# Differential attention of 8 heads: two value steps together behind score 4, the others behind scores 10 and 12

## The chip, the cores and the metric

The kernel runs on one core of a Trainium2 chip. Its time is the device time of one execution in microseconds (us). The core's engines work side by side, each through its own instruction stream in order: TensorE (PE, its weight loads PEld), VectorE (DVE), ScalarE (ACT), GpSimd (POOL) and SyncE (SP, which issues DMAs). They hand work to each other through semaphores.

## The reference

The program is a stack of twelve layers on an input of 4 batches x 512 tokens x 128 channels. The change lies in the eleventh, the differential attention of layer L3: 8 heads, each with two score maps of 8 dimensions, and the second softmax is subtracted with the weight `diff_weight`:

```python
qs = (x @ Wq.T).reshape(b, s, H, 2, F)          # H = 8, F = 8
ks_ = (x @ Wk.T).reshape(b, s, H, 2, F)
vs = (x @ Wv.T).reshape(b, s, H, DH)            # DH = 16
scores = jnp.einsum('bqhif,bkhif->ibhqk', qs, ks_) * scale
atts = jax.nn.softmax(scores, axis=-1)
att = atts[0] - diff_weight * atts[1]
o = jnp.einsum('bhqk,bkhe->bqhe', att, vs)
```

The result is normalised over all channels, projected by `Wo` and added to the stream.

## The kernel before

`diff_attention(kind)` serves two layers; kind 3 is the one with 8 heads, kind 2 the one with 16. In kind 3 the work comes in 16 items (4 batches x 4), each of 4 maps (two heads, two maps each) over 512 queries x 512 keys. The softmax is computed with the true maximum of each row subtracted, and that takes two passes over the scores:

- **Peaks.** `peak(n, i)` (L2090) computes a 128 x 512 block of scores of item n, 16 blocks per item, into one of three PSUM banks (`PEAKS = 3`, L1945). DVE takes the maximum of each row (`reduce`, L2387). Peak i must wait until the reduction of peak i-3 is done. Peaks run 24 blocks (`LEAD`), that is one and a half items, ahead of the scores.
- **Placing.** POOL writes the negated maxima as bfloat16 columns into NM (`negate`, L2551 and L2553), once all 16 reductions of an item are done. PE adds them to the stacked queries through identity matmuls (`place`, L2117 and L2119, two per item) and ACT copies the result to QM (`shift`, L2283).
- **Scores.** `score(n, i)` (L2129), again 16 blocks per item, writes the shifted scores with the keys on the partitions into a ring of four PSUM banks, which placings, gatherings and projections share; ACT takes the exponential into EX (L2276).
- **Values.** `value(n, c)` (L2139), c = 0 to 3, multiplies a quarter of the exponentials by the values, in float32, four maps side by side in column tiles of 32. A step shows in the trace as 8 matmul records. All four steps of an item accumulate into bank 4. They run one item late: during item n the steps of item n-1.
- **Gathering.** ACT takes bank 4 to OT (`take`, L2290), PE turns it (`gather`, L2150), and DVE copies the turned block to OS (`keep`, L2022), once per item from item 2 on. DVE works through its own order: `keep` stands ahead of the ninth reduction of an item.

The loop over an item on PE has 16 places i = 0 to 15. At each stand, in this order: the peaks that `AHEAD_OF` puts there, score i, a placing of the next item (i = 10 and 12), a gathering (i = 6), in items 0, 4 and 8 a projection of the next batch (i = 3 and 7), and a value step where `AT_VALUE` says so. In this text P0 to P15 are the 16 peaks in an item's loop, S0 to S15 its scores, V0 to V3 its value steps. `AHEAD_OF` gives one peak at i = 0, 1, 2, 4, 7 and 8 and two at i = 3, 6, 10, 12 and 14. The last item has tables of its own, `AT_VALUE_LAST` and `AT_VALUE_OWN`.

The lines that the change touches:

```python
AT_VALUE = {2: (4, 7, 11, 14), 3: (4, 8, 10, 14)}[kind]      # L1949
...
values_at = AT_VALUE if n + 1 < items else AT_VALUE_LAST      # L2220
if i in values_at and n:
    value(n - 1, values_at.index(i))
```

Of the kernel before, what the change touches and what calls it, by code (L numbers as in the profile page):

```python
# [128 lines left out]
class Kernel:  # L129
# [1717 lines left out]
    def diff_attention(self, kind):  # L1847
# [89 lines left out]
        def split_at(n):  # L1937

            b, g = divmod(n, per_b)
            return b + 1 if g == {2: 2, 3: 0}[kind] and b + 1 < B else None  # L1940
# [5 lines left out]
        LEAD = 24 // PW  # L1946
        AHEAD_OF = {2: (0, 0, 1, 2, 3, 4, 5, 5, 7, 8, 9, 11, 11, 12, 13, 14), 3: (0, 1, 2, 3, 3, 4, 6, 6, 7, 8, 10, 10, 12, 12, 14, 14)}[kind]
        AT_PLACE = {2: (9,), 3: (10, 12)}[kind]
        AT_VALUE = {2: (4, 7, 11, 14), 3: (4, 8, 10, 14)}[kind]  # L1949
        AT_VALUE_LAST = (1, 3, 5, 6)  # L1950
        AT_VALUE_OWN = (9, 11, 14)
        AT_TAKE = 0
# [7 lines left out]
        def ended(n):  # L1960

            return n // GROUP if n >= 0 and n % GROUP == GROUP - 1 else None
# [16 lines left out]
        def bank_of(u):  # L1979
            return banks[RING[turn[u] % len(RING)]]  # L1980
# [25 lines left out]
        def at16(name, n, i):  # L2006
            return S[name].at(16 * n + i + 1)
# [17 lines left out]
        with nc.Block() as block:  # L2025
# [44 lines left out]
            def _(pe):  # L2070
                def bank_free(u):

                    r = turn[u]
                    if r < len(RING):
                        return
                    user = ring[r - len(RING)]
                    if user[0] == "score":
                        pe.wait_ge(S["exp"].sem, at16("exp", user[1], user[2]))
                    elif user[0] == "place":
                        pe.wait_ge(S["shifted"].sem, S["shifted"].at(stacks * user[1] + user[2] + 1))  # L2080
                    elif user[0] == "gather":
                        pe.wait_ge(S["kept"].sem, S["kept"].at(user[1] + 1))
                    else:
                        pe.wait_ge(S["qk_rest"].sem, S["qk_rest"].at(2 * user[1] + user[2] + 1))

                def project(b, s, out):
                    pe.matmul(out, WQK[:, s, :], nT[:, b * L:(b + 1) * L], start=True, stop=True
                              ).then_inc(S["qk_proj"].sem, 1)

                def peak(n, i):  # L2090
                    qt, jp = divmod(i, 4 // PW)
                    if n == 0 and i == 0:
                        pe.wait_ge(quarter.sem, quarter.at(16 * 2 * slots))
                    if n == per_b // 4 and i == 0:
                        pe.wait_ge(stacked[0].sem, stacked[0].at(16 * 2 * slots))
                    if n and n % (per_b // 2) == 0 and i == 0:
                        b, h = divmod(2 * n // per_b, 2)
                        half = stacked[b % 2 * 2 + h]
                        pe.wait_ge(half.sem, half.at(16 * 2 * slots * (b // 2 + 1)))
                    if kind == 2 and i == 0 and n == 0:  # L2100
                        pe.wait_ge(zeroed.sem, zeroed.at(slots))
                    if kind == 2 and i == 0 and n == per_b:
                        pe.wait_ge(filled.sem, filled.at(2 + slots))
                    if PK * n + i >= PEAKS:
                        pe.wait_ge(S["reduced"].sem, at_peak("reduced", n, i - PEAKS))
                    for k in range(PW):
                        r, buf, g, m = where(n, MAPS[PW * jp + k])
                        last = pe.matmul(peaks_at(PK * n + i)[:, k, :], QS[r, buf, g, qt * P:(qt + 1) * P], KM[r, buf, g, m, :],  # L2108
                                         start=True, stop=True)
                    last.then_inc(S["peak"].sem, 1)  # L2110

                def place(n, s):
                    pe.wait_ge(S["negated"].sem, S["negated"].at(n + 1))
                    bank_free(("place", n, s))
                    out = bank_of(("place", n, s))
                    _, buf, g, _ = where(n, s * slots)
                    pe.matmul(out, self.identb[:], QS[:, buf, g, :], start=True, stop=False)  # L2117
                    for qt in range(TB):
                        last = pe.matmul(out[:, qt * P:(qt + 1) * P], NM[:, qt, s * P:(s + 1) * P],  # L2119
                                         self.identb[:], start=False, stop=qt == TB - 1)  # L2120
                    last.then_inc(S["placed"].sem, 1)

                def score(n, i):
                    kt, at = divmod(i, 4)
                    if i == 0:
                        pe.wait_ge(S["shifted"].sem, S["shifted"].at(stacks * (n + 1)))
                    bank_free(("score", n, i))
                    r, buf, g, m = where(n, MAPS[at])
                    pe.matmul(bank_of(("score", n, i)), KM[r, buf, g, m, kt * P:(kt + 1) * P],  # L2129
                              QM[r, n % 2, MAPS[at] // slots, :], start=True, stop=True).then_inc(S["score"].sem, 1)  # L2130

                def value(n, c):
                    pe.wait_ge(S["exp"].sem, at16("exp", n, 4 * c + 3))
                    if c == 0:
                        pe.wait_ge(S["vstage"].sem, S["vstage"].at(n + 1))
                        if n and n % GROUP == 0:
                            pe.wait_ge(S["taken"].sem, S["taken"].at(n // GROUP))
                    for j in range(4):
                        last = pe.matmul(banks[4][32 * j:32 * j + 32, :], VST[:, n % 2, c, j // 2, :],  # L2139
                                         EX[n % 2][:, c, j, :], start=c == 0 and n % GROUP == 0,  # L2140
                                         stop=c == TB - 1 and ended(n) is not None)
                    if c == TB - 1:
                        last.then_inc(S["value"].sem, 1)

                def gather(u):
                    pe.wait_ge(S["taken"].sem, S["taken"].at(u + 1))
                    bank_free(("gather", u, 0))
                    out = bank_of(("gather", u, 0))
                    for qt in range(TB):
                        last = pe.transpose(out[:, qt * P:(qt + 1) * P], OT[:, qt * P:(qt + 1) * P], self.ident[:])  # L2150
                    last.then_inc(S["gathered"].sem, 1)
# [9 lines left out]
                def turn_rows(b):  # L2161
                    if b == 0:
                        pe.wait_ge(S["reduced"].sem, S["reduced"].at(PK * items))
                    pe.wait_ge(S["post"].sem, S["post"].at(6 * b + 4))
                    out = banks[b if b + 1 < B else 4]
                    for j in range(TB):
                        last = pe.transpose(out[:, j * P:(j + 1) * P], ON[:, b * TB + j, :], self.ident[:])
                    last.then_inc(turned.sem, 1)
# [37 lines left out]
                for n in range(items):  # L2206
                    for i in range(16):
                        for p in range(PK * n + LEAD, min(PK * (n + 1) + LEAD, PK * items)):
                            if AHEAD_OF[p - PK * n - LEAD] == i:
                                peak(*divmod(p, PK))  # L2210
                        score(n, i)
                        if i in AT_PLACE and n + 1 < items:
                            place(n + 1, AT_PLACE.index(i))
                        if i == AT_GATHER and ended(n - 2) is not None:
                            gather(ended(n - 2))
                        if i in AT_PROJECT and split_at(n) is not None:
                            u = ("project", split_at(n), AT_PROJECT.index(i))
                            bank_free(u)
                            project(u[1], u[2], bank_of(u))
                        values_at = AT_VALUE if n + 1 < items else AT_VALUE_LAST  # L2220
                        if i in values_at and n:
                            value(n - 1, values_at.index(i))
                        if n + 1 == items and i in AT_VALUE_OWN:
                            value(n, AT_VALUE_OWN.index(i))
                        if kind == 3 and n == items - 1 and i in AT_TURN:
                            turn_rows(AT_TURN.index(i))
# [925 lines left out]
```

## Time and profile before

| | us |
|---|---|
| median of 3 runs | 1703.02 (1702.91 to 1708.54) |
| the profiled execution | 1702.36 |
| its span | 1700.5 |
| PE busy in the span | 1432.8 (84%) |
| DVE busy | 1198.5 (70%) |
| ACT busy | 1111.8 (65%) |

The span is the time between the first and the last instruction that the profiler recorded; the execution's time has 1.86 us more around it. A row of the timeline gives the start in the span, the length, the engine, the line, the operation with its tiles, how many like instructions follow each other, and in brackets how long the engine had been idle before and who released it. Rows of one engine that follow each other closely overlap a little in the record, so the pace of an engine is better read from start to start than from the length of one instruction. Matmuls of different tiles overlap on PE, and their ends are modelled. The stretch of the attention with 8 heads in which all engines work runs from about 1430 to 1600 us.

### The profile page before, as it was taken

To read this page: it belongs to the slowest core of one execution; us is meant where nothing else is said; L and a number is where in the kernel's file an instruction comes from. 1 tells how busy PE (TensorE), PEld (TensorE's weight loads), DVE (VectorE), ACT (ScalarE), POOL (GpSimd) and SP (SyncE) were. 2 spreads that over 40 slices of the span, in tenths; PEclk is the share of its full clock that TensorE was granted. 3 is DMA by queue.
4 is the path that set the end of the run, shared out by engine and by line. 5 is a ranking of instruction groups with operands and counts; after the bars stand their busy time and mean duration, and the time that the engine had idled before them with its cause. 6 is when DMAs were issued, how large, how long until landed. Compare 5 with 4: busy or idle time off the path is not lost. (4 is left out here: it accounts for less than half of the span.)

```text
span 1700.5 us, 29624 instructions
## 1 busy us (share of the span) xinstructions
PE 1432.8 (84%) x9239; PEld 833.1 (49%) x9239; DVE 1198.5 (70%) x2827; ACT 1111.8 (65%) x2522; POOL 460.1 (27%) x610
## 2 busy tenths in 40 slices
PE   4798668999999695884799999998578887999979
PEld 4355564777777594784222222223477452222255
DVE  6477645877788746325999999995622767999566
ACT  3454556988888573444489898985444444888833
POOL 1231434433433242652130202011364000221100
PEclk8698787999999797987799999999789897999979
DMA  2002214220300243112330304002111204222000
GB/s 83 5 1 100 76 54 119 59 60 16 75 1 1 62 133 112 43 42 75 87 88 1 87 2 107 1 1 103 49 43 61 74 18 129 74 74 62 1 1 25
DMA packets 75077, 93.81 MB, mean 55 GB/s; under 512 B 11200, under 2 KB 61504, under 8 KB 74544
## 3 DMA queue, kind: packets, MB, share of 16 engines
q1 hardware_dynamic: 67088, 77.27, 16.0%
q0 software_dynamic: 6144, 12.60, 2.6%
q10 hardware_dynamic: 1696, 2.10, 0.6%
q8 instruction: 77, 1.26, 0.3%
q14 instruction: 72, 0.59, 0.1%
HBM read 57.22 MB, written 34.70 MB: 54 GB/s over the span
## 5 line engine op out<-in xcount | busy, mean ns | idle before, releaser
L2387 DVE TENSOR_REDUCE MAXI<-psum 128x1 f32<-128x512 f32 x768 | 473.0, 683 | 36.0 <-PE psum L2108 31.8
L2276 ACT ACTIVATE BIG<-psum 128x512 f32<-128x512 f32 x768 | 410.8, 609 | 61.1 <-PE psum L2129 54.6
L2108 PE MATMUL psum<-KM,QS 64*128 64x512 bf16 x768 | 254.5, 401 | 42.0 <-DVE MAXI L2387 25.9
L2129 PE MATMUL psum<-QM,KM 64*128 64x512 bf16 x768 | 233.2, 386 | 2.2 <-DVE REST L2377 1.9
L2139 PE MATMUL psum<-BIG,VST 128*32 128x512 f32 x1536 | 204.6, 604 | 4.9 <-ACT OT L2290 4.2
L2974 DVE TENSOR_TENSOR LOWS<-EX,HIGHS 128x1024 fp32r<-128x1024 f32 x128 | 158.2, 1240 | 61.5 <-POOL HIGHS L3030 31.9
L1215 PE MATMUL psum<-m_XT,m_W 128*128 128x128 f32 x992 | 145.3, 294 | 27.7 <-DVE m_XT L1482 22.6
L2108 PEld LDWEIGHTS psum<-KM,QS 64*128 64x128 bf16 x768 | 56.8, 94 | 223.3 <-DVE MAXI L2387 194.6
L2916 ACT ACTIVATE EX<-psum 128x512 f32<-128x512 f32 x256 | 153.7, 608 | 18.0 <-PE psum L2831 18.0
L3030 POOL CAST HIGHS<-EX 128x512 fp32r<-128x512 f32 x128 | 109.1, 852 | 179.2 <-ACT EX L2916 114.7
L1215 PEld LDWEIGHTS psum<-m_XT,m_W 128*128 128x128 f32 x992 | 132.0, 207 | 36.0 <-DVE m_XT L1482 28.1
L1229 PE MATMUL psum<-BIG,m_H 128*128 x992 | 135.4, 282 | 0.3
L1493 DVE SCALAR_TENSOR_TENSOR m_Y<-psum,m_MASK,m_Y 128x128 f32 x124 | 43.5, 351 | 125.6 <-PE psum L1229 105.4
L2551 POOL CAST NM<-MAXI 128x16 bf16<-128x16 f32 x48 | 12.2, 254 | 428.7 <-DVE MAXI L2387 428.7
L1229 PEld LDWEIGHTS psum<-BIG,m_H 128*128 128x128 f32 x992 | 125.5, 199 | 0.8 <-issue 0.7
L1176 POOL DMA_INDIRECT m_XG<-rows,m_ROWS x96 | 93.1, 970 | 111.2 <-DVE m_ROWS L1417 52.9
L1184 POOL DMA_INDIRECT y<-m_Y,m_ROWS x96 | 93.7, 976 | 79.8 <-DVE m_Y L1493 70.7
L2842 PE MATMUL psum<-HIGHS,NH 128*128 128x512 f32 x256 | 110.0, 430 | 0.0
L1329 ACT ACTIVATE m_H<-psum 128x512 f32<-128x512 f32 x78 | 46.4, 594 | 93.6 <-PE psum L1215 60.5
L1310 ACT ACTIVATE m_W<-BIG 128x512 f32 x124 | 78.6, 634 | 42.0 <-DVE m_PLACE L1431 38.9
L2129 PEld LDWEIGHTS psum<-QM,KM 64*128 64x128 bf16 x768 | 56.9, 93 | 96.0 <-ACT BIG L2276 82.8
L2844 PE MATMUL psum<-HIGHS,NL 128*128 128x512 f32 x256 | 101.6, 397 | 0.0
(363 smaller groups left out, 2557.2 us busy)
## 6 DMA issues: line engine op xcount, KB each, us to landing
BIG<-in_w_dram SPq DMA_DIRECT2D x24, 512.0 KB
parts<-PART SPq DMA_DIRECT2D x24, 384.0 KB, 2.6
parts<-PART SPq DMA_DIRECT2D x24, 256.0 KB, 2.3
rows<-N SPq DMA_DIRECT2D x16, 256.0 KB, 2.7
N<-y SPq DMA_DIRECT2D x16, 256.0 KB, 4.0
QS<-parts SPq DMA_DIRECT2D x32, 128.0 KB, 3.9
QS<-parts SPq DMA_DIRECT2D x14, 256.0 KB, 5.8
parts<-PART SPq DMA_DIRECT2D x24, 128.0 KB, 1.8
```

Source lines behind the costliest of these rows:

```text
L1215: last = pe.matmul(up_banks[r % len(up_banks)][:, it * P:(it + 1) * P], W[:, r % DEEP, it * P:(it + 1) * P], XT[:, r % XS, :], start=True, ...
L1229: last = pe.matmul(down_at(r), H[:, r % HS, it * P:(it + 1) * P], DOWN[:, bass.ds(e, 1), it * P:(it + 1) * P].rearrange("p e n -> p (e n)" ...
L2108: last = pe.matmul(peaks_at(PK * n + i)[:, k, :], QS[r, buf, g, qt * P:(qt + 1) * P], KM[r, buf, g, m, :], start=True, stop=True)
L2129: pe.matmul(bank_of(("score", n, i)), KM[r, buf, g, m, kt * P:(kt + 1) * P], QM[r, n % 2, MAPS[at] // slots, :], start=True, stop=True).th ...
L2139: last = pe.matmul(banks[4][32 * j:32 * j + 32, :], VST[:, n % 2, c, j // 2, :], EX[n % 2][:, c, j, :], start=c == 0 and n % GROUP == 0, s ...
L2276: act.activation(EX[n % 2][:, kt, MAPS[j], :], bank_of(("score", n, i)), ACT.Exp, scale=SM_SCALE).then_inc(S["exp"].sem, 1)
L2387: dve.tensor_reduce(MAXI[:, n % 2, qt, columns], peaks_at(PK * n + i), AX, ALU.max, negate=True).then_inc(S["reduced"].sem, 1)
L2842: pe.matmul(banks[4 + j], NH[:, t, :], HIGHS[:, pair(n, kt), j, :], start=kt == 0, stop=False)
L2844: last = pe.matmul(banks[4 + j], NL[:, t, :], HIGHS[:, pair(n, kt), j, :], start=False, stop=kt == TB - 1)
L2916: act.activation(EX[:, kt, j, :], bank_of(("score", n, i)), ACT.Exp, scale=SM_SCALE, accum_out=SUMS[:, n % 2, j, kt:kt + 1]).then_inc(S["e ...
L2974: dve.tensor_tensor(LOWS[:, pair(n, kt)], EX[:, kt], HIGHS[:, pair(n, kt)], ALU.subtract).then_inc(S["low"].sem, 1)
L3030: pool.tensor_copy(HIGHS[:, pair(n, kt), 0, :], EX[:, kt, 0, :]).then_inc(S["high"].sem, 1)
```

## The change

It changes the table of kind 3 from (4, 8, 10, 14) to (4, 4, 10, 12), and the loop that reads it, so that one place may hold two steps. Kind 2 keeps its table. The second step is issued at once behind the first at i = 4, the third stays behind the first placing, and the fourth goes from behind score 14 to behind the second placing. The table holds for items 1 to 14; item 0 has no value steps and item 15 its own tables. No instruction is added or removed, and the streams of ACT, DVE, POOL and SP stand as before.

```diff
-        AT_VALUE = {2: (4, 7, 11, 14), 3: (4, 8, 10, 14)}[kind]
+        AT_VALUE = {2: (4, 7, 11, 14), 3: (4, 4, 10, 12)}[kind]
...
                         values_at = AT_VALUE if n + 1 < items else AT_VALUE_LAST
-                        if i in values_at and n:
-                            value(n - 1, values_at.index(i))
+                        for k, at in enumerate(values_at):
+                            if at == i and n:
+                                value(n - 1, k)
```

PE's stream in an item without projection, from P5 (peaks read KM and QS) on. L2129 are scores, L2150 a gathering, L2139 the value steps, of four matmul instructions each. Before:

```order
L2108 MATMUL psum<-KM,QS 128x512
L2129 MATMUL psum<-QM,KM 128x512
L2139 MATMUL psum<-BIG,VST 32x512 x4
L2129 MATMUL psum<-QM,KM 128x512
L2108 MATMUL psum<-KM,QS 128x512 x2
L2129 MATMUL psum<-QM,KM 128x512
L2150 MATMUL psum<-ident,OT 128x128 x4
L2108 MATMUL psum<-KM,QS 128x512
L2129 MATMUL psum<-QM,KM 128x512
L2108 MATMUL psum<-KM,QS 128x512
L2129 MATMUL psum<-QM,KM 128x512
L2139 MATMUL psum<-BIG,VST 32x512 x4
```

The same place in the changed kernel (the first row is again P5):

```order
L2108 MATMUL psum<-KM,QS 128x512
L2129 MATMUL psum<-QM,KM 128x512
L2139 MATMUL psum<-BIG_2,VST 32x512 x8
L2129 MATMUL psum<-QM,KM 128x512
L2108 MATMUL psum<-KM,QS 128x512 x2
L2129 MATMUL psum<-QM,KM 128x512
L2150 MATMUL psum<-ident,OT 128x128 x4
L2108 MATMUL psum<-KM,QS 128x512
L2129 MATMUL psum<-QM,KM 128x512
L2108 MATMUL psum<-KM,QS 128x512
L2129 MATMUL psum<-QM,KM 128x512 x2
L2108 MATMUL psum<-KM,QS 128x512 x2
```

Eight value matmuls now stand between S4 and S5, and between S8 and S9 there are none. BIG and BIG_2 are the two halves of EX that the items use in turn.

The second half of an item on PE, from the first placing (L2117 and L2119) to the fourth value step. Before:

```order
L2117 MATMUL psum<-QS,identb 128x512
L2119 MATMUL psum<-identb,NM 128x128 x4
L2139 MATMUL psum<-BIG,VST 32x512 x4
L2129 MATMUL psum<-QM,KM 128x512
L2108 MATMUL psum<-KM,QS 128x512 x2
L2129 MATMUL psum<-QM,KM 128x512
L2117 MATMUL psum<-QS,identb 128x512
L2119 MATMUL psum<-identb,NM 128x128 x4
L2129 MATMUL psum<-QM,KM 128x512
L2108 MATMUL psum<-KM,QS 128x512 x2
L2129 MATMUL psum<-QM,KM 128x512
L2139 MATMUL psum<-BIG,VST 32x512 x4
```

The same in the changed kernel:

```order
L2117 MATMUL psum<-QS,identb 128x512
L2119 MATMUL psum<-identb,NM 128x128 x4
L2139 MATMUL psum<-BIG_2,VST 32x512 x4
L2129 MATMUL psum<-QM,KM 128x512
L2108 MATMUL psum<-KM,QS 128x512 x2
L2129 MATMUL psum<-QM,KM 128x512
L2117 MATMUL psum<-QS,identb 128x512
L2119 MATMUL psum<-identb,NM 128x128 x4
L2139 MATMUL psum<-BIG_2,VST 32x512 x4
L2129 MATMUL psum<-QM,KM 128x512
L2108 MATMUL psum<-KM,QS 128x512 x2
L2129 MATMUL psum<-QM,KM 128x512 x2
```

The fourth value step now stands ahead of S13, P14, P15 and S14 instead of behind them.

## Rows read from the trace of the kernel before

**Rows 1.** Windows of 1430 to 1620: start:end, length, busy us of each engine, granted clock

```profile
1430.00:1460.00 30.00, 27.08 (x171) 7.59 (x173) 27.42 (x46) 25.96 (x51) 6.88 (x13) 0.94 0.48 123
1460.00:1490.00 30.00, 28.44 (x201) 8.29 (x197) 27.37 (x46) 27.29 (x54) 6.18 (x10) 1.00 0.23 72
1600.00:1620.00 20.00, 17.41 (x126) 7.41 (x126) 3.19 (x13) 13.30 (x25) 0.00 (x0) 1.00 0.00 1
```

**Rows 2.** Timeline of DVE, from the keeping of item 2 to that of item 5

```profile
1456.73 0.43 DVE L2022 COPY OS<-psum 128x272 f32<-128x272 f32 x1
1457.08 2.48 DVE L2387 TENSOR_REDUCE MAXI<-psum 128x1 f32<-128x512 f32 x4
1460.26 7.63 DVE L2387 TENSOR_REDUCE MAXI<-psum 128x1 f32<-128x512 f32 x12 [0.71 <-PE psum L2108]
1467.81 0.43 DVE L2022 COPY OS<-psum 128x272 f32<-128x272 f32 x1
...
1479.66 0.43 DVE L2022 COPY OS<-psum 128x272 f32<-128x272 f32 x1
...
1480.92 0.69 DVE L2387 TENSOR_REDUCE MAXI<-psum 128x1 f32<-128x512 f32 x1 [0.23 <-PE psum L2108]
...
1484.35 7.63 DVE L2387 TENSOR_REDUCE MAXI<-psum 128x1 f32<-128x512 f32 x12 [0.79 <-PE psum L2108]
1491.90 0.43 DVE L2022 COPY OS<-psum 128x272 f32<-128x272 f32 x1
```

**Rows 3.** Timeline of PE, items 2 and 3, around the value steps

```profile
1458.26 0.39 PE L2117 MATMUL psum<-QS,identb 128*128 128x512 bf16 x1
...
1458.81 1.07 PE L2139 MATMUL psum<-BIG,VST 128*32 128x512 f32 x8
...
1459.81 0.60 PE L2108 MATMUL psum<-KM,QS 64*128 64x512 bf16 x2
...
1462.42 0.39 PE L2129 MATMUL psum<-QM,KM 64*128 64x512 bf16 x1
...
1464.83 0.39 PE L2108 MATMUL psum<-KM,QS 64*128 64x512 bf16 x1 [0.21 <-DVE MAXI L2387]
...
1465.14 1.06 PE L2139 MATMUL psum<-BIG,VST 128*32 128x512 f32 x8
1466.14 0.39 PE L2129 MATMUL psum<-QM,KM 64*128 64x512 bf16 x1
...
1466.68 0.65 PE L2150 MATMUL psum<-ident,OT 128*128 128x128 f32 x4
1467.27 0.39 PE L2108 MATMUL psum<-KM,QS 64*128 64x512 bf16 x1
...
1467.80 0.64 PE L2139 MATMUL psum<-BIG,VST 128*32 128x512 f32 x4
```

**Rows 4.** Timeline of POOL at the keeping of item 4

```profile
1479.81 0.26 POOL L2551 CAST NM<-MAXI 128x16 bf16<-128x16 f32 x1 [9.82 <-DVE MAXI L2387]
1480.14 0.27 POOL L2553 TENSOR_TENSOR NM<-MAXI,NM 128x16 bf16<-128x16 f32 x1
```

**Rows 5.** Timeline of ACT, item 3, and two rows of item 14

```profile
1464.29 2.09 ACT L2276 ACTIVATE BIG<-psum 128x512 f32<-128x512 f32 x4
1466.57 1.75 ACT L2276 ACTIVATE BIG<-psum 128x512 f32<-128x512 f32 x3 [0.18 <-PE psum L2129]
...
1595.38 1.09 ACT L2276 ACTIVATE BIG<-psum 128x512 f32<-128x512 f32 x2 [0.23 <-PE psum L2129]
...
1597.24 1.08 ACT L2276 ACTIVATE BIG<-psum 128x512 f32<-128x512 f32 x2 [0.29 <-PE psum L2129]
```

## The prediction

> **What bounds the kernel now.** I read the windows first, to see whether one engine is simply full. In the attention with 8 heads none is: in a stretch of 30 us PE is busy 28.44, DVE 27.37 and ACT 27.29 [rows 1]. So the order of the work decides, and the timelines have to be read item by item. DVE shows an item best, because its keeping comes once in each: from 1456.73 to 1467.81 an item takes 11.08 us [rows 2]. Its own work is less. Four reductions in a row take 2.48 us, so they follow each other in (2.48 - 0.68) / 3 = 0.60 us (0.68 is the length of a single one), and from a keeping to the next reduction it is 0.35 us [rows 2]. 16 x 0.60 + 0.35 = 9.95 us. The 1.13 us that are left are one gap of 0.78 ahead of P12's reduction (the fourth of the row at 1457.08 ends its turn at 1457.08 + 4 x 0.60 = 1459.48, the next starts at 1460.26) and 0.35 spread over the row of 12 (its 11 steps take 7.63 - 0.68 = 6.95 us where 11 x 0.60 = 6.60).
>
> PE's timeline says who makes whom wait [rows 3]. Take V0's start, 1465.14, as zero. From V0 on PE has no long wait: S5 follows at 1.00, the gathering at 1.54, P8 at 2.13, V1 at 2.66; one item earlier (V0 at 1465.14 - 11.08 = 1454.06) the first placing starts at 4.20, V2 at 4.75, P12 at 5.75. From S15 (1462.42, that is 8.36) to the next V0 at 11.08 it takes 2.72 us for 12 matmuls, waiting for DVE (0.21 ahead of P5) to give back one of three peak banks. Four such matmuls take 0.54 (S5 to the gathering), so twelve take 1.6: PE has 1.1 us of slack in its item, all at i = 0 to 4, and P5 is issued the moment P2's reduction ends. A value step holds PE for 1.00 us.
>
> **The change part by part.** Three things move per item; nothing is added.
>
> *V1 behind V0.* At V0 DVE holds three peaks at most. P2's turn ends at -0.35, so P3, P4 and P5 last it until -0.35 + 1.80 = 1.45. P6 now starts behind V0 and S5 at 1.01, and its reduction 0.45 later (P12 was issued at 1459.81 and its reduction started at 1460.26 [rows 2, 3]), at 1.46: just in time, which is why no gap shows there. With two steps PE reaches P6 at 2.00 and DVE starts it at 2.45: a new gap of 1.00 us. What the second step costs behind a first is not in the trace. The row that is cut off after four records has 0.64, whole ones 1.07, so the second four add 0.43, and a step alone could take 0.86 of streaming; the pair lies between 1.72 + 0.14 = 1.86 and 2 x 1.00. I take 2.00, which is the row itself, and keep 0.14 for the range.
>
> *V1 away from behind S8.* From P6's reduction at 2.45 DVE ends P7 at 3.65, keeps until 4.00 (the gathering starts at 2.54 and lasts 0.65, in time) and ends P8 at 4.60. PE comes to P11 at about 3.7, but P11 needs P8's bank: it waits until 4.64. Its wait stands where V1 stood. From P10 and P11 to the first placing it is 0.35 us, to V2 another 0.55, V2 1.00: placing 5.0, V2 5.55, P12 6.55, its reduction 7.00. DVE has ended P9, P10 and P11 at 6.40: gap 0.60 (before 0.78). The placing also needs POOL's negated maxima: POOL casts 0.15 us after the keeping's start and is done at 1480.14 + 0.27 = 1480.41, 0.75 behind 1479.66 [rows 2, 4], so at 3.65 + 0.75 = 4.40 here, hidden by P11's wait; without that cover the placing would be about 0.3 later than PE's own pace.
>
> *V3 ahead of S13, P14 and P15.* P12 and P13 are reduced from 7.00 to 8.20. PE goes through the second placing (0.55) and now V3 (1.00) before P14: the step from P12 to P14 is 0.53 + 0.55 + 1.00 = 2.08, so P14 comes at 8.63 and its reduction at 9.08: a new gap of 0.88 us. In its old place V3 had P12 to P15 issued ahead of it, and DVE ran through. After it DVE is unbroken: P14, P15 and P0 to P2 end at 12.08, P5 follows at 12.1 and V0 at 12.43.
>
> Sum for DVE: 9.95 + 1.00 + 0.60 + 0.88 = 12.43 us per item, 1.35 more than 11.08. The small waits of 0.35 are gone, since P0 no longer stands behind V3. ACT is not later than this: now S4's exponential ends at about 1.24 (1464.29 + 2.09 = 1466.38) and S5's starts at 1.43 after a wait of 0.18 [rows 5]. With the pair S5's starts at 2.43, and from there ACT has work only as PE gives it; its 16 exponentials, two shifts and one taking (4 in 2.09, that is about 0.55 each, so 19 x 0.55 = 10.5 us) fit in 12.4.
>
> How many items: the table holds for items 1 to 14. Eleven are as computed (1 to 13 without 4 and 8): 11 x 1.35 = 14.9 us. Items 4 and 8 have the two projections. Around item 4 the two intervals take 11.85 + 12.24 us, 1.93 above two plain ones, and show gaps of 0.23 and 0.79 [rows 2]. There the projection at i = 7 feeds DVE late and takes the place of P11's wait, and the gap ahead of P12 closes, since two REST subtractions and the keeping fill it; the pair and V3 open about 1.0 and 0.7. Net 1.7 - 1.0 = 0.7, twice 1.4. The bounds are 0 and 1.35 each. Item 14 has peaks only up to P7; there ACT waits 0.18, then 0.23 and 0.29 behind value steps [rows 5], and would wait 1.0 and 0.4 instead: +0.7 (bounds 0 and 1.35). Item 15 is unchanged, and nothing later depends on when it ends but by shift. 14.9 + 1.4 + 0.7 = 17.0 us.
>
> On two steps in a row: the row shows 1.00 us from V0 to S5, of which 0.86 is streaming, so leaving the column tiles costs 0.14 [rows 3]. The Trainium skill, TensorEngine Tiling (Array Packing), Key Properties, says that a change of the tiling mode drains TensorE. By that rule the pair saves one such change, and the sum would be 13 x 0.14 = 1.8 us lower.
>
> The profiled execution took 1702.36, so 1719.4; the median stands 0.66 above it. I predict **1720 us**, about 1% slower.
>
> **The rivals.**
>
> *R1: only the pair costs.* If V3's gap stays closed, an item takes 12.43 - 0.88 = 11.55, +0.47, and the time is 1702.4 + 13 x 0.47 = 1708.5, say 1709. For it: small waits could merge. Against: three banks are all that DVE can have in hand, and 2.08 us stand against 1.20 of reductions.
>
> *R2: PE is the bound and gets cheaper.* If PE's busy time set the pace, the order would matter only by what the tile changes cost. One entry and exit less per item is 0.14 plus a like price at most, 0.2 us: 14 x 0.2 = 2.8, 1699.6. For it: PE is 95% busy [rows 1]. Against: 1.1 us of slack at i = 0 to 4. The rule of the skill named above is what this rival lives from.
>
> *R3: the slack takes V1 in, faster.* PE's slack of 1.1 us stands at i = 0 to 4, and V1 needs 1.0: moved there it leaves the stretch i = 5 to 15, in which PE never waits, 1.0 us shorter, and DVE's gap of 0.78 closes: 13 x 0.78 = 10.1, 1692.3. It decides if DVE has work for the 2.00 + 0.31 + 0.45 = 2.76 us from P5 to P6's data. Three banks hold 1.80, so it would need five. That speaks strongly against it.
>
> *R4: the clock falls.* PE's busy share falls by more than a tenth. The granted clock is 1.00 in 1460 to 1490, and still 1.00 at 17.41 of 20 us, but 0.94 in 1430 to 1460 [rows 1]. If two items ran at the lower level of 1.2 GHz, PE's 9.9 us of work would about double, past 12.4 by 7: +14, 1734. The Trainium skill, TensorE: Matmul & The Clock Gate, on cycling through PSUM banks, says that short idles between groups of matmuls can make the clock swing; by that rule this rival would be likelier, while the row with 87% busy at 1.00 speaks against.
>
> That the change does something else than it says I leave out: PE's stream shows the eight value matmuls in a row in items 1 to 14.
>
> **How the numbers follow.** Forecast 77%, with a range of its own from 1714 (pair 0.14 cheaper, projection items and item 14 at nothing, 0.1 us per item of misread waits) to 1725 (these at 1.35 each, and some trace of the clock). R1 7%, R2 6%, R3 5%, R4 5%. The range 1708 to 1727 takes in the forecast and R1 and leaves out R2 to R4. A measurement of this kernel can tell about 0.5% (8.5 us) from no change: faster than 1694.5 is R3, 5%; within it are R2 and R1, 13%; slower 82%.
>
> **What would show it.** On DVE an item from keeping to keeping takes 12.3 to 12.5 us, with three gaps: one of about 1.0 ahead of P6's reduction, that is two reductions ahead of each keeping, one of 0.6 ahead of P12, one of 0.9 ahead of P14, all released by PE. On PE the pair takes 1.86 to 2.0, and a wait for DVE of nearly 1 us stands ahead of P11. On ACT a wait of 1.0 stands ahead of S5. The prediction is wrong if items stay near 11.1 (then R2 or a cheaper pair), if only one new gap is there (R1), or if items outside 1 to 14 or the granted clock change (R4).

## The result and the profile after

| | before | after |
|---|---|---|
| median, us | 1703.02 (5 runs, 1698.21 to 1708.54) | 1726.14 (5 runs, 1724.97 to 1733.25) |
| ratio | | 1.0141, 95% interval 1.0116 to 1.0165 |
| profiled execution, us | 1702.36 | 1724.97 |
| span, us | 1700.5 | 1723.2 |

The change makes the kernel 1.4% slower. I had forecast 1720, between 1708 and 1727. By the ratio the time stands at 1703.02 x 1.0141 = 1727.03, just above the range; by its interval it lies between 1722.8 and 1731.1. The direction and the three gaps came out as written; the size was 17 us in the forecast and 23 to 24 in the measurement.

The timeline of DVE in the changed kernel answers to [rows 2]. It goes from the keeping of item 2 to that of item 5 (the columns are those of [rows 2]; line numbers are one higher than before):

```profile
1460.85 0.43 DVE L2022 COPY OS<-psum 128x272 f32<-128x272 f32 x1
1461.20 2.48 DVE L2388 TENSOR_REDUCE MAXI<-psum 128x1 f32<-128x512 f32 x4
1464.26 1.29 DVE L2388 TENSOR_REDUCE MAXI<-psum 128x1 f32<-128x512 f32 x2 [0.58 <-PE psum L2108]
1466.34 4.88 DVE L2388 TENSOR_REDUCE MAXI<-psum 128x1 f32<-128x512 f32 x8 [0.79 <-PE psum L2108]
1472.11 1.29 DVE L2388 TENSOR_REDUCE MAXI<-psum 128x1 f32<-128x512 f32 x2 [0.90 <-PE psum L2108]
1473.32 0.43 DVE L2022 COPY OS<-psum 128x272 f32<-128x272 f32 x1
...
1486.56 0.43 DVE L2022 COPY OS<-psum 128x272 f32<-128x272 f32 x1
...
1500.31 0.43 DVE L2022 COPY OS<-psum 128x272 f32<-128x272 f32 x1
```

The unbroken row of twelve reductions is cut into groups of 2, 8 and 2. The gaps stand ahead of P12 (0.58, forecast 0.60), P14 (0.79, forecast 0.88) and P6 (0.90, forecast 1.00). The brackets count from the end of a record of 0.68 us, the forecast from the end of a turn of 0.60, so about 0.08 has to be added to each before the two are compared. An item takes 1473.32 - 1460.85 = 12.47 us, forecast 12.43, before 11.08.

PE's timeline of item 3 in the changed kernel answers to [rows 3]:

```profile
1469.80 1.92 PE L2139 MATMUL psum<-BIG,VST 128*32 128x512 f32 x16
...
1471.65 0.39 PE L2129 MATMUL psum<-QM,KM 64*128 64x512 bf16 x1
...
1473.46 0.39 PE L2108 MATMUL psum<-KM,QS 64*128 64x512 bf16 x1
...
1474.40 0.39 PE L2108 MATMUL psum<-KM,QS 64*128 64x512 bf16 x1 [0.56 <-DVE MAXI L2388]
...
1475.27 1.06 PE L2139 MATMUL psum<-BIG,VST 128*32 128x512 f32 x8
...
1477.35 1.06 PE L2139 MATMUL psum<-BIG,VST 128*32 128x512 f32 x8
```

The pair of value steps is one row of 16, and S5 follows 1.85 us after its start. P10 starts at 1473.46 and P11 at 1474.40: this is the wait for P8's bank, where V1 had been. The trace counts 0.56 us of it as idle and names DVE's reduction as what ended it.

Two things stand beside the gaps. First, the changed kernel came to item 0 later: the first REST subtraction there (DVE's part of a projection) started at 1435.60 against 1433.51, 2.09 us, before any instruction that the change moves. It was 2.03 us late already at the subtraction that stands at 1402.50 (before 1400.47). That is within the spread of executions of one kernel (1698.21 to 1708.54 before). Second, one interval is too long. Windows around item 9's pair (start:end, length, busy us of each engine, granted clock):

```profile
1500.00:1540.00 40.00, 36.77 (x246) 10.60 (x242) 33.91 (x58) 31.91 (x63) 8.03 (x17) 1.00 0.19 48
...
1550.00:1552.00 2.00, 2.00 (x12) 0.22 (x4) 0.12 (x1) 0.00 (x0) 0.00 (x0) 0.50 1.03 215
```

and the timeline there:

```profile
1548.71 3.47 PE L2139 MATMUL psum<-BIG,VST 128*32 128x512 f32 x16
...
1552.67 1.29 DVE L2388 TENSOR_REDUCE MAXI<-psum 128x1 f32<-128x512 f32 x2 [2.54 <-PE psum L2108]
```

The granted clock fell to the lower of its levels (0.50, 1.2 GHz) during the pair, which took 3.47 instead of 1.92 us, and DVE's gap grew from 0.90 to 2.54: 1.64 us. The same happened once more at the value steps of item 15, which is not changed itself (the keeping of item 15 came 13.52 us after that of item 14, before 11.88). V0 of item 15, before and then changed:

```profile
1601.41 1.06 PE L2139 MATMUL psum<-BIG,VST 128*32 128x512 f32 x8 [1.60 <-ACT OT L2290]
1623.55 1.51 PE L2139 MATMUL psum<-BIG,VST 128*32 128x512 f32 x8 [1.66 <-ACT OT L2291]
```

It started 7.34 us after the keeping of item 14 (before 7.23), and item 15's keeping came 6.18 us behind it (before 4.65): item 14 cost 0.11 and this fall 1.53. In the kernel before, the windows from 1440 to 1616 show 1.00.

### The profile page after: what moved, and what is told of

Read it like the earlier page. It is cut to its first block and busy times, and to the rows that moved or that the text cites. A ratio compares the mean times of both kernels' runs of the same rounds, so it can differ in the third digit from the quotient of the medians.

```text
span 1723.2 us, 29624 instructions
## 1 busy us (share of the span) xinstructions
PE 1445.1 (84%) x9239; PEld 832.9 (48%) x9239; DVE 1198.7 (70%) x2827; ACT 1112.7 (65%) x2522; POOL 461.1 (27%) x610
## 5 line engine op out<-in xcount | busy, mean ns | idle before, releaser
L2108 PE MATMUL psum<-KM,QS 64*128 64x512 bf16 x768 | 260.1, 404 | 46.7 <-DVE MAXI L2388 31.1
L2129 PE MATMUL psum<-QM,KM 64*128 64x512 bf16 x768 | 236.8, 389 | 2.9 <-DVE REST L2378 1.9
L2139 PE MATMUL psum<-BIG,VST 128*32 128x512 f32 x1536 | 204.5, 611 | 4.9 <-ACT OT L2291 4.2
L1215 PE MATMUL psum<-m_XT,m_W 128*128 128x128 f32 x992 | 144.7, 293 | 28.9 <-DVE m_XT L1482 22.7
L2129 PEld LDWEIGHTS psum<-QM,KM 64*128 64x128 bf16 x768 | 57.0, 94 | 90.8 <-ACT BIG L2277 62.1
```

What stands on the lines that cost most here:

```text
L1215: last = pe.matmul(up_banks[r % len(up_banks)][:, it * P:(it + 1) * P], W[:, r % DEEP, it * P:(it + 1) * P], XT[:, r % XS, :], start=True, ...
```

## The experiments

The times of the kernel before differ between the chips, so each run is compared with the kernel before on its own chip (1675.35 for the four runs of the tables, 1708.29 for the banks and the repetition, 1676.78 for the last three). The intervals from one keeping to the next are sharper: in the two profiles of the changed kernel they repeat to 0.01 us. A plain interval is one of an item without projection, without a summing step of DVE and without a fall of the clock.

| run | ratio to before (95%) | plain interval, us | the two around item 4 |
|---|---|---|---|
| before | | 11.08 | 11.85, 12.24 |
| changed | 1.0141 (1.0116 to 1.0165) | 12.47 | 13.24, 13.75 |
| changed, again | 1.0157 (1.0127 to 1.0188) | 12.47 | 13.24, 13.75 |
| pair only (4, 4, 10, 14) | 1.008 (1.0055 to 1.0105) | 11.80 | 12.58, 13.09 |
| fourth step only (4, 8, 10, 12) | 1.0083 (1.0052 to 1.0115) | 11.73 | 12.51, 12.90 |
| changed, old table in items 4 and 8 | 1.0128 (1.0103 to 1.0154) | 12.47 | 12.38, 13.09 |
| (3, 7, 10, 14) | 1.0033 (1.002 to 1.0046) | 10.93 | 12.57, 13.34 |
| four peak banks, old table | 1.0082 (1.005 to 1.0114) | 11.69 | 12.76, 13.50 |
| four peak banks, new table | 1.0115 (1.0079 to 1.015) | 12.12 | 13.17, 14.54 |
| changed, wait filled | 1.0131 (1.0111 to 1.0151) | 12.70 | 13.48, 13.79 |
| old table, second step left out | 1673.0 us, a single run | 10.95 | 11.73, 12.22 |
| (3, 7, 10, 14), old table in items 4 and 8 | 0.9984 (0.997 to 0.9998) | 10.93 | 11.73, 12.22 |

**The two parts of the change, each alone.**

```diff
-3: (4, 4, 10, 12)
+3: (4, 4, 10, 14)
```

> Table (4, 4, 10, 14): the second value step behind the first, the fourth in its old place. Theory (three peak banks give VectorE 1.8 us of reductions in hand, and every stretch of TensorE work longer than that opens a gap): the gaps of about 0.9 ahead of P6 and 0.6 ahead of P12 stay, the one of 0.79 ahead of P14 goes, a wait of 0.2 to 0.35 comes back ahead of P0. An item takes 11.65 to 11.75 us, +0.6 against 11.08, 13 items: +7 to +9 us, 1710 to 1712. Rival (the loss comes from the pair alone, the fourth step is free): the time of the changed kernel, 1724 to 1727.

```diff
-3: (4, 4, 10, 12)
+3: (4, 8, 10, 12)
```

> Table (4, 8, 10, 12): the fourth value step behind the second placing, the other three in their old places. Theory: the gap of 0.78 ahead of P12 stays, one of 0.79 opens ahead of P14, and the small waits of 0.35 in the row of twelve go in part: an item takes 11.5 to 11.6 us, 13 items: +6 to +7 us, 1708 to 1710. Rival (the fourth step has slack around it and is free): 1702 to 1704, no gap ahead of P14.

DVE in a plain item of the first:

```profile
1545.28 2.47 DVE L2388 TENSOR_REDUCE MAXI<-psum 128x1 f32<-128x512 f32 x4
1548.34 6.29 DVE L2388 TENSOR_REDUCE MAXI<-psum 128x1 f32<-128x512 f32 x10 [0.59 <-PE psum L2108]
1555.54 1.29 DVE L2388 TENSOR_REDUCE MAXI<-psum 128x1 f32<-128x512 f32 x2 [0.90 <-PE psum L2108]
```

and of the second:

```profile
1552.73 2.47 DVE L2388 TENSOR_REDUCE MAXI<-psum 128x1 f32<-128x512 f32 x4
1555.91 1.29 DVE L2388 TENSOR_REDUCE MAXI<-psum 128x1 f32<-128x512 f32 x2 [0.71 <-PE psum L2108]
1558.00 6.20 DVE L2388 TENSOR_REDUCE MAXI<-psum 128x1 f32<-128x512 f32 x10 [0.79 <-PE psum L2108]
```

Each part makes its own gap: the pair 0.90 ahead of P6, the fourth step 0.79 ahead of P14. Both rivals (all in the pair, the fourth step free) fall. The plain items took 11.80 and 11.73 us, a little more than I had expected (11.65 to 11.75, 11.5 to 11.6). The medians stand 12.0 and 10.5 us above before, expected 7 to 9 and 6 to 7: from the keeping of item 2 to that of item 14 it is 145.8 us in both, 8.3 above the 137.45 of before. The rest lies outside this stretch (item 1, a fall of the clock at item 15 in the second run, the spread between executions) and was not taken apart. In the intervals the parts add up: +0.72 and +0.65 give +1.37, measured +1.39.

**What V1 had cost where it stood.**

```diff
 def value(n, c):
+    if kind == 3 and c == 1 and n < items - 2:
+        return
```

with the old table, so a quarter of the value product is missing in items 0 to 13.

> The kernel before, but the second value step is left out in items 0 to 13, so a quarter of the value product is missing. It measures what V1 cost where it stood. Theory (V1 stood in a wait of TensorE for P8's reduction): only the gap ahead of P12 shrinks, from 0.78 to about 0.6, an item takes 10.9 us. Rival (V1 costs its 1.0 us on TensorE): 10.1 to 10.3 us.

```profile
1545.21 2.47 DVE L2390 TENSOR_REDUCE MAXI<-psum 128x1 f32<-128x512 f32 x4
1548.27 7.62 DVE L2390 TENSOR_REDUCE MAXI<-psum 128x1 f32<-128x512 f32 x12 [0.59 <-PE psum L2108]
1555.81 0.43 DVE L2022 COPY OS<-psum 128x272 f32<-128x272 f32 x1
```

P11 on PE in the same item:

```profile
1545.94 0.39 PE L2108 MATMUL psum<-KM,QS 64*128 64x512 bf16 x1 [0.56 <-DVE MAXI L2390]
```

An item takes 10.95 us without the step, 0.13 less than with it, about as expected (10.9). A step that holds PE for 1.00 us cost 0.13 of it behind S8, because PE stands there waiting for P8's reduction: the row of P11 shows the same wait as in the changed kernel. The rival (10.1 to 10.3) falls.

**The items with projections.**

```diff
 values_at = AT_VALUE if n + 1 < items else AT_VALUE_LAST
+if kind == 3 and n in (4, 8):
+    values_at = (4, 8, 10, 14)
```

> The changed kernel, but items 4 and 8, which have the projections, keep the old table (4, 8, 10, 14). It measures the term of the sum that came out too small (0.7 predicted for each of these items). Theory: these items cost 1.5 each in the changed kernel, because the first placing waits for the second REST subtraction without V1 to fill the wait; the time is 3 us below the changed kernel. By the predicted term it would be 1.4 us below.

The two intervals around item 4 fall from 13.24 + 13.75 = 26.99 to 12.38 + 13.09 = 25.47 us. Item 4 cost 1.52 in the changed kernel, and items 4 and 8 together 3.06: from the keeping of item 2 to that of item 14 it is 152.30 us against 155.36, with one fall of the clock in that stretch in both. The ratios, 1.0128 and 1.0141, are too close for their intervals to tell 3 us from the 1.4 that I had predicted. One row of PE in item 4 of the changed kernel shows where a part of it lies:

```profile
1489.26 0.38 PE L2117 MATMUL psum<-QS,identb 128*128 128x512 bf16 x1 [1.04 <-DVE REST L2378]
```

The first placing takes the ring bank that the second projection used, and waits 1.04 us for its subtraction. In the kernel before V1 stood between the two, and the placing behind it waited for nothing:

```profile
1480.82 1.07 PE L2139 MATMUL psum<-BIG,VST 128*32 128x512 f32 x8
...
1482.36 0.39 PE L2117 MATMUL psum<-QS,identb 128*128 128x512 bf16 x1
```

DVE's gaps ahead of P12 and P14 are then 0.94 and 0.79 in the changed kernel (the gap ahead of P12 was 0.79 before [rows 2]):

```profile
1491.24 1.29 DVE L2388 TENSOR_REDUCE MAXI<-psum 128x1 f32<-128x512 f32 x2 [0.94 <-PE psum L2108]
1493.33 4.88 DVE L2388 TENSOR_REDUCE MAXI<-psum 128x1 f32<-128x512 f32 x8 [0.79 <-PE psum L2108]
```

With the old table in item 4 the gap ahead of P12 is 0.79 again:

```profile
1464.83 6.29 DVE L2390 TENSOR_REDUCE MAXI<-psum 128x1 f32<-128x512 f32 x10 [0.79 <-PE psum L2108]
```

**More banks for the peaks.**

```diff
-PEAKS = 2 if PAIRED else 3
+PEAKS = 2 if PAIRED else {2: 3, 3: 4}[kind]
-RING = (5, 6, 7) if PAIRED else (5, 6, 7, 3)
+RING = (5, 6, 7) if PAIRED or kind == 3 else (5, 6, 7, 3)
...
-(0, 1, 2, spare[0])
+(0, 1, 2, 3)
```

> Four PSUM banks for the peaks of the attention with 8 heads in place of three, and three in the ring for scores in place of four; the table of before (4, 8, 10, 14). Theory: VectorE has 2.4 us of reductions in hand, the gap of 0.78 ahead of P12 shrinks to 0.2; an item takes 10.5 to 10.9 us unless the shorter ring holds the scores back: 2 to 7 us faster than before on the same chip. Rival (the ring of three binds ScalarE): 3 to 12 us slower.

> The same four peak banks with the changed table (4, 4, 10, 12). Theory (the loss is the reach of the peak banks): each of the three gaps shrinks by the 0.60 of one more reduction, to 0.3, 0 and 0.2, so the loss against the old table with four banks falls from 22 us to between 0 and 8. Rival (the order costs TensorE time by itself, whatever the banks): the loss stays at 17 to 22 us.

The medians are 1719.89 and 1728.44, 8.6 us apart, against 1733.16 - 1708.29 = 24.9 on the same chip with three banks. The loss shrank by two thirds, just above the 0 to 8 that I had expected, and far from the rival's 17 to 22. But the gaps did not do what I had written. DVE in a plain item with the new table:

```profile
1588.31 2.48 DVE L2388 TENSOR_REDUCE MAXI<-psum 128x1 f32<-128x512 f32 x4
1591.09 1.29 DVE L2388 TENSOR_REDUCE MAXI<-psum 128x1 f32<-128x512 f32 x2 [0.31 <-PE psum L2108]
1593.17 4.88 DVE L2388 TENSOR_REDUCE MAXI<-psum 128x1 f32<-128x512 f32 x8 [0.79 <-PE psum L2108]
1598.87 1.29 DVE L2388 TENSOR_REDUCE MAXI<-psum 128x1 f32<-128x512 f32 x2 [0.82 <-PE psum L2108]
```

Only the gap ahead of P12 shrank (0.58 to 0.31), because PE no longer waits for P8's bank. The one ahead of P14 stayed at 0.79: DVE is empty when P12 comes, gets two peaks and runs dry, however many banks there are. The one ahead of P6 stayed at 0.82. Between P14 and V0 PE now waits for ACT to free a bank of the ring, which is one way to a late P6; that it is the whole of the 0.82 is not shown:

```profile
1593.88 0.37 PE L2129 MATMUL psum<-QM,KM 64*128 64x512 bf16 x1 [0.34 <-ACT BIG L2277]
```

The old table got worse with this split (11.69 against 11.08, ratio 1.0082), as its rival said: 11.6 us of median, where the rival had 3 to 12. So a good part of the smaller loss is that the base lost too; on this chip the new table with four banks is 4.7 us faster than with three. The 8.6 us also hold two falls of the clock (items 6 and 7, 13.76 us each where a plain one takes 12.12): by the plain intervals the new table costs 0.43 with four banks and 1.39 with three. The trial supports the account for P11 and P12 alone; a fourth peak bank without taking one from the scores was not tried, since all eight are in use.

**The falls of the clock.**

> The changed kernel once more, for a second profile. Plain items take 12.46 us again and items 4 and 8 add 1.5 each (these are set by the order). The two drops of the granted clock inside the attention, which cost 1.6 us each in the first profile, come from the free running of the clock and not from the order: theory, they stand in other places or are missing, and the time moves by as much; rival, they stand again in items 9 and 15.

The interval up to item 9's keeping is 15.38 us again, with the same gap:

```profile
1555.50 1.29 DVE L2388 TENSOR_REDUCE MAXI<-psum 128x1 f32<-128x512 f32 x2 [2.54 <-PE psum L2108]
```

and item 15's is 13.52 again. My theory for this run (they stand in other places or are missing) fell: both stand where they stood.

To see whether the idle time makes them, I filled it:

```diff
+def filler(u, count):
+    bank_free(u)
+    for _ in range(count):
+        pe.matmul(bank_of(u).rearrange("p (m t) -> p m t", t=P), self.UPTOB[:],
+                  self.identb[:].unsqueeze(1).broadcast_to([P, 4, P]), start=True, stop=True)
...
+# ahead of P11, plain items: filler(("place", n + 1, 0), 3); items 4, 8: ahead of the first placing
```

> The changed kernel with three more matmuls of 512 columns (0.22 us each, their result is overwritten) in the wait of TensorE ahead of P11 in the plain items, and ahead of the first placing in items 4 and 8. Theory: the order of the changed kernel leaves TensorE idle for 0.9 us or more there, the lower clock in item 9 (15.38 us in both profiles where its neighbours take 13.75 and 12.47) comes from these idle times, and the filler takes it away at no cost: plain items 12.47 again, item 9's interval 13.75, 1.6 to 3.3 us faster than the changed kernel. Rival (the drop does not depend on idle time there): interval 15.4 again, no gain, or slower by the filler's 0.65 us per item.

Item 9 is free of the fall (13.79 us), but one stands in item 11 instead (14.35 us where a plain one takes 12.70), with the clock at 0.50:

```profile
1549.00:1551.00 2.00, 2.00 (x12) 0.22 (x4) 0.66 (x2) 0.00 (x0) 0.00 (x0) 0.50 0.00 0
```

and item 15's is still there (13.50). The filler itself costs 0.23 us in each plain item (12.70). The run was inconclusive: what PE does before moves the fall, but it is not shown that the idle time which I filled is the cause. The other profiles say where to look. The old table in items 4 and 8 alone moved the fall from item 9 to item 12 (14.11 us against 12.46) and kept the one in item 15 (13.57). The fourth step alone had one in item 15 (13.76), the four banks with the new table had two, in items 6 and 7. So all six profiles with the fourth step at i = 12 have a fall in items 2 to 15. The six with it at i = 14 (before, pair only, both with (3, 7, 10, 14), second step left out, four banks with the old table) have none there. The falls go with the fourth step's place, in one profile of each kernel (two of the changed one); through what is not shown. How busy PE is does not tell them apart by itself: in the filled run it was busy 44.03 of the 47 us from 1500 on, ahead of the fall, in the kernel before 56.24 of the 60 us from 1440 on, without one.

**A better order.**

> Table (3, 7, 10, 14): the first two value steps one place earlier, none together. Theory: V0 goes into the stretch where TensorE waits for peak banks (i = 0 to 4), between P4 and P5, with two reductions in hand and one place given up, V1 between P8 and P9; no stretch between two peaks is longer than 1.8 us there and the gap ahead of P12 shrinks from 0.78 to about 0.4: an item takes 10.6 to 10.8 us, 4 to 6 us faster than before, 1697 to 1699. Rival (V0 comes too early and waits for the taking of the item before): as before or slower, 1703 to 1710, with a wait of TensorE ahead of V0.

The edit is the table (3, 7, 10, 14). The plain interval fell to 10.93 us, 0.15 less than before, not the 0.3 to 0.5 that I had expected, and the two intervals around item 4 rose by 0.72 and 1.10: 0.33% slower in all, where I had expected 4 to 6 us faster. A value step directly behind a projection makes the long stretch that the table avoids elsewhere. DVE's two gaps in item 4:

```profile
1450.12 0.69 DVE L2388 TENSOR_REDUCE MAXI<-psum 128x1 f32<-128x512 f32 x1 [1.06 <-PE psum L2108]
...
1454.91 0.69 DVE L2388 TENSOR_REDUCE MAXI<-psum 128x1 f32<-128x512 f32 x1 [1.37 <-PE psum L2108]
```

The same table with the old one in items 4 and 8:

```diff
-3: (4, 4, 10, 12)
+3: (3, 7, 10, 14)
...
+if kind == 3 and n in (4, 8):
+    values_at = (4, 8, 10, 14)
```

> Table (3, 7, 10, 14) in the plain items, the table of before in items 4 and 8. In the run of (3, 7, 10, 14) everywhere the plain intervals took 10.93 us (11.08 before), but those around items 4 and 8 12.57 and 13.34 (11.85 and 12.24 before). Theory: the loss came from a value step next to a projection alone, so here ten or so intervals gain 0.15 each and none loses: 1 to 2 us faster than before (ratio 0.999). Rival (the moved steps pass their delay into items 4 and 8 whatever their own table): 2 to 5 us slower.

1673.29 us against 1676.78, ratio 0.9984 (0.997 to 0.9998): the interval just excludes no change. From the keeping of item 2 to that of item 14 it is 136.3 us, 1.15 less than before, within the 1 to 2 us that I had expected; the rival falls. This version beats both kernels, by little.

## Why the prediction was right and where it was too small

*What bounds the kernel.* Right. No engine is full, DVE gives the pace, and a long stretch of PE between two peaks opens each gap [rows 2, 3].

*V1 behind V0.* Counted as the forecast counts, in turns of 0.60 us, the gap is 0.97 against 1.00, and two errors that nearly cancel make it so, which is luck. I had taken two single steps of 1.00; the pair takes 1.85 us from its start to S5, the lower of my two bounds (1.86), so P6's reduction starts 2.31 behind V0 and not 2.45. But DVE ran dry at 1.34 (1466.34 + 8 x 0.60 = 1471.14, less 1469.80) and not at 1.45: P2's turn had ended 0.14 ahead of P5's issue, where I had taken 0.04. The 0.14 by which the prediction's sentence on two steps in a row made the pair cheaper came out in its number; that the reason is the one given there is not shown.

*V1 away from behind S8.* Right: a gap of 0.58, by turns 0.66 (1464.26 - 1461.20 - 4 x 0.60, forecast 0.60), and P11's wait where V1 stood. The run without V1 shows it from the other side.

*V3 ahead of P14.* Right: 0.79, by turns 0.88, the forecast. PE takes from P12 to P14 exactly 2.08 us (1476.27 to 1478.35), and DVE's two turns 1.20.

*The sum per item.* 12.47 against 12.43. The three gaps by turns give 0.97 + 0.66 + 0.88 = 2.51 (forecast 2.48), and 9.95 + 2.51 = 12.46.

*How many items.* The failure lies here and in the clock. From V0 of item 1 to the keeping of item 14 the changed kernel lost 22.03 - 2.09 = 19.94 us (1594.18 to 1616.21, less the 2.09 that it came late). 1.64 of it is the clock. The other 18.30 stand against my 17.0:
- Item 1 up to the keeping of item 2 grew by 2.03 us, six plain intervals by 8.47, 1.41 each (1.35 forecast); one of them 1.52, since it had been 10.95.
- Two intervals that hold a summing step of DVE (items 7 and 11) grew by only 0.94 each: that step now falls into a gap. I had not looked at them apart.
- **The term of the order that failed is that of items 4 and 8.** I had 0.7 each, because the gap ahead of P12 was to close there. It did not close: it was 0.79 before and 0.94 in the changed kernel. The two intervals around item 4 grew by 1.39 + 1.51 = 2.90, around item 8 3.02; without the plain interval in each pair that is 1.5 to 1.6, and undoing it gave 1.52. I had let the projection at i = 7 take over V1's part as cover, and not followed the bank that it used: the placing behind it waits for the REST subtraction. It is above my bound of 1.35, too.
- Item 14: I had 0.7, and it cost 0.11 up to V0 of item 15.

*The clock, R4: the larger part of the miss.* **The sum of 17.0 put the clock at nothing**; only the upper end of the forecast's own range had some trace of it. I had given R4 5% and a price of 14 us as a case against the forecast, and had named a changed clock as a sign that the prediction is wrong. It came beside the forecast, at a quarter of that price: two falls of 1.64 and 1.53 us, 3.2 in all. The order took 18.4, the clock 3.2 and the late start 2.1, together 23.7; behind the attention the profile won 1.0 back, which makes the 22.7 by which the spans differ. Order and clock alone are 21.6 us, inside the 19.8 to 28.1 that the interval of the ratio gives; the rest of the distance to 24 is no more than executions of one kernel differ by. So the steps that failed are the clock at 0 instead of 3.2 us and items 4 and 8 at 1.4 instead of 3.1, partly made good by item 14 at 0.7 instead of 0.1.

*R1 to R3.* Each would have shown as a missing gap; all three gaps are there. The table (3, 7, 10, 14), which has V0 at i = 3 in PE's slack at i = 0 to 4 (R3), gives 0.15 per plain item; it moves V1 by a place too, and the two were not tried apart.

## What to carry to other kernels

When two engines share work through a few buffers, count for each stretch of the producer between two hand-overs how long it is, and how much work the consumer has in hand at its start; the difference is the gap, and it can be read to a tenth of a microsecond from a timeline of before. An instruction that seems to cost its full time may stand in a wait and cost an eighth of it, so moving it away uncovers the wait and takes a second place for itself. Work the odd items (with projections, first, last) out one by one, bank by bank: items 4 and 8 made the largest error among the gaps here, 1.7 us. A new order can also come with falls of the granted clock, 3.2 us here: put a term for them into the sum and its range, not only a rival.

## What the runs showed of the hardware that I had not expected

- Two value steps in a row (16 matmul records of float32 in column tiles of 32) take 1.85 us until the next score, where one (8 records) takes 1.00.
- The granted clock fell to 0.50 (1.2 GHz) with PE busy: in the 3 us window around item 9's pair in the repetition PE was busy throughout, and in the 60 us from 1440 to 1500 it was busy 52.59 us at 1.00.

```profile
1440.00:1500.00 60.00, 52.59 (x350) 15.27 (x356) 50.17 (x84) 49.87 (x99) 13.03 (x23) 1.00 0.32 88
1552.00:1555.00 3.00, 3.00 (x18) 0.57 (x12) 0.95 (x2) 0.56 (x2) 0.00 (x0) 0.50 1.03 220
```

- The fall stands at the same item in two profiles of the same kernel, and costs the same 1.64 us. It came in the six profiles with the fourth step at i = 12 and in none of the six with it at i = 14. What in the order sets it off stays open.
